# Scores of two heads at once on the row halves of TensorE's array, ahead of the value products

## The reference

```python
qh = (q @ Wq).reshape(b, l, HEADS, HEAD_DIM).transpose(0, 2, 1, 3)   # l = 128
kh = (kv @ Wk)...; vh = (kv @ Wv)...                                  # s = 2048
qh = rms_norm(qh, q_norm_w); kh = rms_norm(kh, k_norm_w)
scores = jnp.einsum('bhld,bhsd->bhls', qh, kh) * (1.0 / np.sqrt(HEAD_DIM))
scores = jnp.where(mask, scores, NEG_INF)          # keys beyond the batch's length
attn = jax.nn.softmax(scores, axis=-1)
o = jnp.einsum('bhls,bhsd->bhld', attn, vh)
x = x + o.reshape(b, l, HEADS * HEAD_DIM) @ Wo
```

## Time and profile before

| | |
|---|---|
| Median of 3 runs | 1441.21 us (1439.97 to 1441.74) |
| Profiled execution | 1442.03 us, its span 1440.3 us |
| TensorE matmul busy | 1230.4 us (85%) |
| VectorE, ScalarE, GpSimd busy | 870.4, 743.7, 821.5 us |
| Mean granted TensorE clock | 0.932 |

### The profile page before, as it was taken

How to read it: one execution, slowest core, us unless ns; L and a number is a source line. 1 busy time by engine, 2 the same in 40 slices (tenths; PEclk the granted TensorE clock), 3 DMA queues, 4 the chain that set the end, 5 groups by cost and what they waited for, 6 DMA issues and landing times. The chain is left out here.

```text
span 1440.3 us, 30819 instructions
## 1 busy us (share of the span) xinstructions
PE 1230.4 (85%) x11696; PEld 1025.7 (71%) x11696; DVE 870.4 (60%) x1880; ACT 743.7 (52%) x1222; POOL 821.5 (57%) x699
## 2 busy tenths in 40 slices
PE   4669999989999999999999999995798855479418
PEld 3548888878888888888888888873587744368316
DVE  5846555576555577555576555553767668587573
ACT  4534666666666667566666666564533331123550
POOL 3516777767777768777767777774501126276210
PEclk9889999999999999999999999996999977779759
DMA  5044667797766798767688767667510022032000
GB/s 177 30 125 85 116 117 120 129 186 130 117 115 118 119 187 155 115 114 119 121 177 144 116 119 121 114 117 152 193 45 1 1 96 88 1 88 59 0 0 30
DMA packets 427554, 149.68 MB, mean 104 GB/s; under 512 B 408208, under 2 KB 408208, under 8 KB 427280
## 3 DMA queue, kind: packets, MB, share of 16 engines
q1 hardware_dynamic: 427408, 147.71, 52.7%
HBM read 45.94 MB, written 1.05 MB: 33 GB/s over the span
## 5 line engine op out<-in xcount | busy, mean ns | idle before, releaser
L358 PE MATMUL pair<-wkv_hi,ctx_hi 128*128 128x256 f16 x2048 | 560.5, 274 | 14.7 <-DVE ctx_lo L541 14.7
L360 PE MATMUL pair<-wkv_hi,ctx_lo 128*128 128x256 f16 x2048 | 560.3, 274 | 0.0
L359 PE MATMUL pair<-wkv_lo,ctx_hi 128*128 128x256 f16 x2048 | 560.3, 274 | 0.0
L566 DVE CUSTOM_DVE_ANT_0 probs<-bank,mask 128x512 f32<-128x512 f32 x256 | 176.7, 690 | 291.3 <-PE bank L636 282.9
L487 POOL TENSOR_TENSOR k_rinv<-k_ms,half_neg 128x8 f32<-128x8 f32 x128 | 212.7, 1662 | 206.3 <-DVE k_ms L585 204.8
L477 POOL TENSOR_TENSOR p_parts<-probs,p_parts 128x512 f16<-128x512 f32 x256 | 291.9, 1158 | 49.2 <-ACT p_parts L522 48.7
L358 PEld LDWEIGHTS pair<-wkv_hi,ctx_hi 128*128 128x128 f16 x2048 | 200.9, 98 | 67.5 <-DVE ctx_lo L541 16.4
L359 PEld LDWEIGHTS pair<-wkv_lo,ctx_hi 128*128 128x128 f16 x2048 | 201.1, 98 | 50.0
L360 PEld LDWEIGHTS pair<-wkv_hi,ctx_lo 128*128 128x128 f16 x2048 | 201.1, 98 | 24.0
L526 ACT ACTIVATE k_lh<-k_n 128x512 f16<-128x512 f32 x128 | 80.5, 629 | 205.8 <-DVE k_n L591 205.2
L515 ACT ACTIVATE probs<-probs,neg_max 128x512 f32<-128x512 f32 x256 | 182.9, 714 | 1.3 <-DVE neg_max L575 1.1
(11 more groups left out here) (244 smaller groups left out, 2048.6 us busy)
## 6 DMA issues: line engine op xcount, KB each, us to landing
ctx_raw<-in_ctx_t_dram SPq DMA_DIRECT2D x64, 256.0 KB, 3.0
cross_out_raw<-in_w_qkv_dram SPq DMA_DIRECT2D x12, 512.0 KB, 4.2
pt<-p_parts SPq DMA_TRANSPOSE x256, 3.3
down_raw<-in_w_down_dram SPq DMA_DIRECT2D x12, 256.0 KB, 2.7
ffn_raw<-in_w_up_dram SPq DMA_DIRECT2D x12, 256.0 KB, 2.8
ffn_raw<-in_w_gate_dram SPq DMA_DIRECT2D x12, 256.0 KB, 2.6
w_raw<-in_wq_dram SPq DMA_DIRECT2D x4, 512.0 KB, 7.9
w_raw<-in_wk_dram SPq DMA_DIRECT2D x4, 512.0 KB, 4.8
```

Of the source, the lines that this page charges most:

```text
L358: nc.tensor.matmul(to, x_hi[k], w_hi[k], start=(k == 0), stop=False)
L359: nc.tensor.matmul(to, x_hi[k], w_lo[k], start=False, stop=False)
L360: mm = nc.tensor.matmul(to, x_lo[k], w_hi[k], start=False, stop=(k == n - 1))
L566: nc.vector.tensor_tensor_reduce(probs[n % PROBS][:, :], scores[:, :], mask[:, k, :], 1.0, LOWEST, ALU.add, ALU.max, chunk_max[head % 2][: ...
```

## The change

The scores of both heads of a pair are computed in one group in every even slot. Each head takes 64 rows of the array: head 0's queries and keys lie on partitions 0 to 63, head 1's on 64 to 127. Three products (hi hi, lo hi, hi lo) per head make six matmuls of 64 rows, alternating between the heads; each head has its own bank. The group stands ahead of the value products. Parts now alternate between the heads. PSUM then holds two `pair`s instead of three, and two banks for the outputs. In `prologue` the stack is [hi, lo] and there is one set of 8 transposes of two heads each, kept by VectorE alone. Lags and buffer counts move.

```diff
-SCORE_LAG, EXP_LAG, PV_LAG = 10, 15, 18
-CTX_RAWS, KTS, VS, PROBS, PTS = 2, 6, 11, 6, 3
+SCORE_LAG, EXP_LAG, PV_LAG = 8, 17, 20
+CTX_RAWS, KTS, VS, PROBS, PTS = 2, 3, 11, 10, 3
...
-        pair = [... psum_tensor(f"pair{i}", [P, 4, 256], F32)) for i in range(3)]
+        pair = [... psum_tensor(f"pair{i}", [P, 4, 256], F32)) for i in range(2)]
+        two = whole.enter_context(nc.psum_tensor("two", [P, 2, 512], F32))
...
 (prologue, tensor)
-                    wait(pe, st_a, m)
-                    for h in range(HH):
-                        mm = nc.tensor.transpose(t_a[:, h * P:(h + 1) * P],
-                                                 stack[m % 2][:, h, 0:2, :]..., ident16[:, :])
+                    wait(pe, st_a, m - 1)
+                    for i in range(HH):
+                        mm = nc.tensor.transpose(t_a[m % 2][:, i * P:(i + 1) * P],
+                                                 stack[m % 2]...[:, i * P:(i + 1) * P], ident16[:, :])
                     mm.then_inc(tr_a, 1)
-                    wait(pe, st_b, m)
-                    for h in range(HH):
-                        mm = nc.tensor.transpose(t_b[:, h * P:(h + 1) * P],
-                                                 stack[m % 2][:, h, 1:3, :]..., ident16[:, :])
-                    mm.then_inc(tr_b, 1)
 (prologue, scalar: keep of t_b is gone; vector: the copy into stack[..., 2, :] is gone)
...
 (cross_attention, vector)
-                    dve.wait_ge(s_done, n + 1)
+                    dve.wait_ge(s_done, n // 2 + 1)
-                    nc.vector.tensor_tensor_reduce(probs[n % PROBS][:, :], scores[:, :], mask[:, k, :], ...
+                    nc.vector.tensor_tensor_reduce(probs[n % PROBS][:, :], scores[h][:, :], mask[:, k, :], ...
...
 (cross_attention, tensor)
                     if slot % 2 == 0:
-                        wait(pe, k_n_done, d - 2)
-                        wait(pe, v_lo_done, d - 2)
+                        wait(pe, k_n_done, d - 1)
+                        wait(pe, v_lo_done, d - 1)
...
+                if (n := part(SCORE_LAG, slot)) is not None and n % 2 == 0:
+                    u, at = n // 8, n // 2
+                    b, group = u // GROUPS, u % GROUPS
+                    pe.wait_ge(kt_in[at % 2], 16 * (at // 2 + 1))
+                    wait(pe, s_max_done, n)
+                    for i, (q_part, k_part) in enumerate(((0, 0), (1, 0), (0, 1))):
+                        for h in range(2):
+                            rows = slice(HD * h, HD * (h + 1))
+                            mm = nc.tensor.matmul(scores[h][:, :], q_st[rows, group // 4 * B + b, q_part, group % 4, :],
+                                                  kt[at % KTS][rows, TILES * k_part:TILES * (k_part + 1), :]...,
+                                                  start=(i == 0), stop=(i == 2))
+                    mm.then_inc(s_done, 1)
                 if (n := part(PV_LAG, slot)) is not None:
-                    u, h, k = n // 8, n // CHUNKS % 2, n % CHUNKS
+                    u, h, k = n // 8, n % 2, n % 8 // 2
...
-                if (n := part(SCORE_LAG, slot)) is not None:
-                    ...
-                    for i in range(2):
-                        mm = nc.tensor.matmul(scores[:, :], q_st[:, group // 4 * B + b, i, 2 * (group % 4) + h, :],
-                                              kt[at % KTS][:, h, :], start=(i == 0), stop=(i == 1))
-                    mm.then_inc(s_done, 1)
```

More of the change, by code:

```diff
@@ L75, in sems @@
             return handles
-        pair = [whole.enter_context(nc.psum_tensor(f"pair{i}", [P, 4, 256], F32)) for i in range(3)]
-        bank = [pair[i // 2][:, 2 * (i % 2):2 * (i % 2) + 2, :].rearrange("p a n -> p (a n)") for i in range(6)]
-        bank += [whole.enter_context(nc.psum_tensor(f"bank{i}", [P, 512], F32)) for i in (6, 7)]
+        pair = [whole.enter_context(nc.psum_tensor(f"pair{i}", [P, 4, 256], F32)) for i in range(2)]
+        bank = [pair[i // 2][:, 2 * (i % 2):2 * (i % 2) + 2, :].rearrange("p a n -> p (a n)") for i in range(4)]
+        bank += [whole.enter_context(nc.psum_tensor(f"bank{i}", [P, 512], F32)) for i in range(4, 6)]
+        two = whole.enter_context(nc.psum_tensor("two", [P, 2, 512], F32))
+        bank += [two[:, i, :] for i in range(2)]
         resid = sb("resid", [P, B, D], F32)
@@ L136, in prologue @@
         q_n, q_w = ([xn[:, 2 * j + i, :].rearrange("p (h d) -> p h d", h=HH) for i in range(2)] for j in range(2))
-        stack = [sb(f"q_stack{i}", [P, HH, 3, HD], F16, c) for i in range(2)]
+        stack = [sb(f"q_stack{i}", [P, 2, HH, HD], F16, c) for i in range(2)]
         x_in, norm_in = sems(c, "x_in norm_in")
@@ L144, in prologue @@
             c, "qp_done sq_done raw_done ss_done ms_done rinv_done qn_done qw_done")
-        hi_done, hi2_done, lo_done, tr_a, tr_b, st_a, st_b = sems(
-            c, "hi_done hi2_done lo_done tr_a tr_b st_a st_b")
+        hi_done, lo_done, tr_a, st_a = sems(c, "hi_done lo_done tr_a st_a")
         q_st = g["q_st"]
-        t_a, t_b = (bank[4 + i].bitcast(F16) for i in range(2))
+        t_a = [bank[4 + i][:, :].bitcast(F16) for i in range(2)]
         block = c.enter_context(nc.Block())
@@ L254, in finish @@
                 act.wait_ge(qw_done, m + 1)
[L256 to L262, removed]
+                wait(act, tr_a, m - 1)
+                nc.scalar.activation(stack[m % 2][:, 0, :, :], q_w[m % 2][:, :, :], ACT.Copy).then_inc(hi_done, 1)
             weights_hi(range(KD))
@@ L268, in _ @@
                                      ACT.Copy).then_inc(x_hi, 1)
-            for n in range(UNITS + 4):
-                if n >= 4:
-                    keep(n - 4)
+            for n in range(UNITS + 2):
                 if n < UNITS:
@@ L370, in cross_attention @@
         ctx_hi, ctx_lo = (sb(n, [P, S // P, KD, P], F16, c) for n in ("ctx_hi", "ctx_lo"))
-        k_sq = sb("k_sq", [P, 2, TILES, HD], F32, c)
+        k_sq = sb("k_sq", [P, TILES, 2, HD], F32, c)
         k_ss = sb("k_ss", [P, 2 * TILES], F32, c)
@@ L374, in cross_attention @@
         k_rinv = [sb(f"k_rinv{i}", [P, 2 * TILES], F32, c) for i in range(2)]
-        k_n = sb("k_n", [P, 2, TILES, HD], F32, c)
-        k_lh = [sb(f"k_lh{i}", [P, 2 * TILES, 2, HD], F16, c) for i in range(2)]
-        kt = [sb(f"kt{i}", [P, 2, CHUNK], F16, c) for i in range(KTS)]
+        k_n = sb("k_n", [P, TILES, 2, HD], F32, c)
+        k_lh = [sb(f"k_lh{i}", [P, 2, CHUNK], F16, c) for i in range(2)]
+        kt = [sb(f"kt{i}", [P, 2 * TILES, P], F16, c) for i in range(KTS)]
         v_hi = [sb(f"v_hi{i}", [P, TILES, 2, VW], F16, c) for i in range(VS)]
@@ L387, in cross_attention @@
         left = sb("left", [P, B, CHUNKS], F32, c)
-        chunk_max = [sb(f"chunk_max{i}", [P, CHUNKS], F32, c) for i in range(2)]
-        head_max = [sb(f"head_max{i}", [P, 1], F32, c) for i in range(2)]
-        neg_max = [sb(f"neg_max{i}", [P, 1], F32, c) for i in range(2)]
+        chunk_max = [sb(f"chunk_max{i}", [P, CHUNKS], F32, c) for i in range(4)]
+        head_max = [sb(f"head_max{i}", [P, 1], F32, c) for i in range(4)]
+        neg_max = [sb(f"neg_max{i}", [P, 1], F32, c) for i in range(4)]
         ctx_in = sems(c, " ".join(f"ctx_in{i}" for i in range(CTX_RAWS)))
@@ L401, in cross_attention @@
         p_done, p_hi_done, p_lo_done, pv_done, o_done = sems(c, "p_done p_hi_done p_lo_done pv_done o_done")
-        pair, scores = g["pair"], bank[6]
-        o_new = bank[7][:, 0:2 * VW].rearrange("p (h v) -> p h v", h=2)
+        pair, scores = g["pair"], bank[4:6]
+        o_new = g["two"][:, :, 0:VW]
         block = c.enter_context(nc.Block())
         def k_of(d):
-            return pair[d % 3][:, :, 0:2 * HD].rearrange("p t (h e) -> p h t e", h=2)
+            return pair[d % 2][:, :, 0:2 * HD].rearrange("p t (h e) -> p t h e", h=2)
         def v_of(d):
-            return pair[d % 3][:, :, 2 * HD:4 * HD].rearrange("p t (h e) -> p t h e", h=2)
+            return pair[d % 2][:, :, 2 * HD:4 * HD].rearrange("p t (h e) -> p t h e", h=2)
         def part(lag, slot):
@@ L552, in _ @@
                 if (n := part(SCORE_LAG + 1, slot)) is not None:
-                    head, k = n // CHUNKS, n % CHUNKS
+                    head, k, h = head_of(n), n % 8 // 2, n % 2
                     b = n // (8 * GROUPS)
-                    if n % (8 * GROUPS) < CHUNKS:
+                    if n % (8 * GROUPS) < 8 and h == 0:
                         if n == 0:
@@ L610, in _ @@
                         pe.wait_ge(ctx_lo_done, b * (S // P) + t + 1)
-                        mm = project(nc, pair[d % 3][:, i, :], [ctx_hi[:, t, k, :] for k in range(KD)],
+                        mm = project(nc, pair[d % 2][:, i, :], [ctx_hi[:, t, k, :] for k in range(KD)],
                                      [ctx_lo[:, t, k, :] for k in range(KD)], [wkv_hi[:, k, group, :] for k in range(KD)],
```

63 lines of the change are left out of this document (29 added, 34 removed).

## The result

The changed kernel takes 1446.26 us (median of 16 runs, 1441.33 to 1450.04) against 1441.47 us before (16 runs); the ratio is 1.0028 (95% interval 1.0019 to 1.0037), so it is 2.7 to 5.3 us slower. The forecast was 1450, 8.8 us (0.6%) slower. The profiled execution took 1444.13 us, 2.1 more than that of before; its mean granted clock is 0.927 against 0.932, so a part of the median's 4.8 may be other executions' clock, which I have not separated.

What follows compares the result with a forecast made beforehand. TensorE's stream of columns was taken to set the pace. Scores -22.9, value products -0.7, prologue -4, start +3, batch changes +2, tail +4 and shape switches +27.6 gave +9.0 us: forecast 1450 us, range 1423 to 1484.

Steps and rivals of the forecast that it cites:

- side by side in three beats: Score matmuls: two heads run at once, 0.65 us per pair of slots; rival of serial heads, 1491 us, chance 0.08.
- a gap at both borders: Before and after the scores' group on TensorE: switching between 128-row and 64-row matmuls costs time, twice per pair of slots.
- no binding of the banks in the steady stretch: Steady cross-attention: projections don't wait for `v_lo`, slack 1.1 us; rival that they do, 1455 us, chance 0.02.
- x: Gap per switch between 128-row and 64-row matmuls on TensorE, put at 0.13 us, between 0 and 0.263.
- The scores' columns: Cross-attention scores: three beats instead of four save 0.216 us in each of 106 pairs of slots, -22.9 us.
- the pairs paced by loads: About 18 pairs of slots at the three changes of batch, where context loads set the pace: no gain counted.
- The change of shape: Switches at the scores' group, two per pair of slots in 106 pairs at 0.13 us: +27.6 us.
- the band that I called no change: Price per switch from 0.074 to 0.101 us, where the time can't be told from before; chance 0.14.
- The full drain with a bare load: Rival: each switch empties TensorE, then loads weights with nothing above them, 0.263 us; 1478 us, chance 0.06.
- Prologue: Stage before cross-attention: fewer transposes, no ScalarE keep or VectorE copy, so it ends earlier; -4 us (-1 to -6).
- Two pairs of banks: Projections wait for `v_lo` of one projection later: +3 us at the start, +2 at batch changes, nothing in the steady stretch.
- Tail: After the last projection: EXP_LAG is 2 larger, so two more parts of 2.09 us are left; +4 us.

Runs made afterwards that it cites:

- e1: Changed kernel with three 128-row score matmuls in place of six 64-row ones (scores no longer the two heads'): 1423.61 us, ratio 0.9869 to the kernel before.
- e2: Changed kernel with the scores' group cut in two around the value products, four changes of shape per pair of slots instead of two: 1466.17 us, ratio 1.0163.
- e3: Changed kernel with both heads' score matmuls on rows 0 to 63, so head 1 gets head 0's scores: 1516.68 us, ratio 1.0513.
- e7: Changed kernel with the six score matmuls ordered head by head instead of alternating: 1444.60 us, ratio 1.0031 to the kernel before.
- e4: Kernel before with its projections waiting as if it had two pairs of banks instead of three: 1445.17 us, ratio 1.0031.
- e8: Changed kernel with the kernel before's lags for exp and value products (15 and 18 instead of 17 and 20): 1447.04 us, ratio 1.0029.
- e11: Kernel before with the scores ahead of the value products in TensorE's order: 1443.65 us, ratio 1.0017.
- e5: Changed kernel with the value products ahead of the scores' group, as in the kernel before: 1445.35 us, ratio 1.0015.

## Why the prediction was off in size

The direction and the mechanism held: side by side in three beats, a gap at both borders, no binding of the banks in the steady stretch, slower in all. The time, 1446.26, is inside the range, which is wide (1423 to 1484) and says little. The loss, 0.28%, is less than half of the 0.6% forecast. The step that failed is the price of a change of shape: x was put at 0.13 us and measures 0.107. Gain and price nearly cancel in this sum, so an error of a fifth in the price halved the result.

The runs close this sum without the profiles. e1 is the changed kernel without borders, so it measures everything but x: 17.8 us under before by the medians (15 to 23 by the interval), where I had 18.6. From e1 to the changed kernel are 22.6 us, where I had 27.6. Together +4.8 instead of +9.0. Term by term:

- *The scores' columns*, -22.9 us: right where TensorE sets the pace. Three beats of 0.216 stand in after, and e1's pair of slots is 0.21 shorter than before's. For the pairs paced by loads I counted no gain, 18 x 0.216 = 3.9 us. That is about right: over the steady pace the three changes of batch take 17.6 us in e1 and 12.5 in before. They take 13.3 in after, 9.0 in e2 and 4.7 in e3 (one execution each): of the changed kernel's forms, the slower a pair of slots is, the more of it hides behind the loads.
- *The change of shape*: the step that was mis-sized. I put x at 0.13 us, between a bare weight load (0.098) and the pipeline (0.165), +27.6 us. Measured: 0.096 and 0.093 at the borders, with 0.03 us of slower beats around them per pair of slots, so 0.107 to 0.108 each in effect: 106 x 2 x 0.107 = 22.7. e1 finds the same by taking them away (22.6 us); e2, from doubling them, 19.9 us. The bare gap lies in the band that I called no change (0.074 to 0.101), the effective price just above it. The full drain with a bare load (0.263) fell.
- *What a border is.* The Trainium skill, TensorEngine Tiling (Array Packing), Key Properties, says that a change of the tiling mode drains TensorE. The trace agrees in part: there is a gap, and no weight load's record crosses it. But the gap from the end of the last beat is 0.10, less than the 0.165 by which a matmul's record outlasts its beat; the projection's record (its end is modelled) still runs when the scores start, so an empty array is not shown. The Trainium skill, TensorE: Matmul & The Clock Gate, Part 3, tells of concurrent tiles, as e3 and after show; it also has matmuls start in strict program order, and I took five beats from that for e7. The runs show three.
- *Prologue*: -4 forecast, -4.5 measured in one pair of executions; the other runs spread by 2 to 3 us.
- *Two pairs of banks*: +3 at the start, +2.4 measured; +2 at the changes of batch, +0.9 in this execution, with signs both ways in the three. e4 gives both together as 3.7 us (2 to 7).
- *Tail*: +4 forecast, +1.9 measured. The longer lag costs nearly what I had: 39.3 us in after against 36.1 with before's lags (e8), 3.2 for two parts. But before's 37.4, with 2.09 us a part, was a long one: e4 and e11, which change nothing there, pass a part in 1.95 and 1.96 us and need 36.0 and 36.1.

That the other terms come so close to e1's 17.8 is partly luck: e1's profiled execution is 20.6 us shorter than before's, with -5.3 in the prologue, +1.7 at the start, -20.2 from slot 8 to the last projection, +1.5 in the tail and +1.8 in the rest of the program, which is unchanged. Between the profiled executions of after and before the difference is 2.1 us instead of the medians' 4.8. A lower mean clock goes with longer executions within the changed kernel's 16 runs (0.933 in the fastest, 0.924 in the slowest). From 110 to 960 us both profiled executions are granted 1.00; from 960 us to the end of the stage it is 0.65 in after and 0.75 before. Whether the lower clock comes from the change is open.

## What to carry to other kernels

Halving a matmul's rows to run two at once pays by beats and costs by borders: here one beat of 0.216 us was saved per two borders of 0.1 us, an even trade, so a group of row-tiled matmuls needs more than one saved beat per visit. Where loads set the pace, a faster loop only waits longer and a slower one less, so gains and losses count for the other stretches alone. A busy share of 100% shows neither the gain nor the gap; set the starts of neighbours against the beat of their columns. And look at where the engine is not full before reshaping where it is: a buffer count, changed from 2 to 4, was worth 18 us in the stretches that the work on the steady loop could not touch.

## What the runs showed of the hardware that I had not expected

Going from 128-row to 64-row matmuls or back leaves a gap of 0.09 to 0.10 us, whether a projection (beat 0.109 us) or a value product (0.03) stands on the other side (after, e2, e5). Matmuls on disjoint rows pair up even when the program lists one head's three first and then the other's (e7): 0.76 us for six with one border, the same as alternating. A 64-row matmul of 512 columns alone takes the 0.216 us of a 128-row one (e3).
